# Two short scans form both halves of the LSTM's hidden state; both tanh results share a PSUM bank

## The chip, the cores and the metric

The kernel runs on one core of a Trainium2 chip. The metric is the device time of one execution in microseconds (us). The engines named below are PE (TensorE; its weight loads are shown apart as PEld), DVE (VectorE), ACT (ScalarE) and POOL (GpSimd); SP is the queue that issues most transfers. They run side by side and wait for one another through semaphores.

## The reference, cut to what matters

The model is a chain of four residual layers over 4096 rows of 128 features: a graph layer, a layer with an LSTM, a second graph layer, and attention with a mixture of experts. The change is in the LSTM, which runs over all 4096 rows as one sequence with one batch row:

```python
def step(carry, xp):
    h, c = carry
    gates = xp + h @ W_hh.T
    i, f, g, o = jnp.split(gates, 4, axis=-1)
    c = jax.nn.sigmoid(f) * c + jax.nn.sigmoid(i) * jnp.tanh(g)
    h = jax.nn.sigmoid(o) * jnp.tanh(c)
    return ((h, c), h)
_, hs = jax.lax.scan(step, (h0, c0), jnp.swapaxes(x_proj, 0, 1))   # 4096 steps, 128 units
```

The kernel writes sigmoid(z) as (1 + tanh(z/2))/2. It keeps 2c in `c_twice` and 2h in `hid_t`, with the factors folded into the weights.

## The kernel before

The stages run one after another: norm and messages, `lstm` (lines 334 to 666), the sums over the sequence, the second graph layer, attention, experts. `lstm` holds the recurrence and, beside it, the first graph layer, whose rows are the LSTM's inputs.

**The recurrence.** A unit of h is a partition. h and W_hh are kept in f16 as a high and a low half each; of the four products the three large ones are computed. So step n has, for each of four gates, two matmuls of one column with the high half of h (`wrec` high, `wrec` low) and one with its low half (`wrec` high). They add onto the input's share, which already lies in PSUM (`gates` for i, f, g; `gate_o` apart). The chain of one step is:

- PE, line 431: when the high half is ready, six matmuls for i, f, g and two for o; when the low half is ready, three for i, f, g, which release ACT, and one for o.
- ACT, line 487: tanh of i, f, g into `tanhs`; line 490: tanh of o into `tanh_o` (in SBUF).
- DVE, line 571: the two products of the cell and their sum, `c_twice`, through the accumulator output.
- ACT, line 493: tanh of c into `tanh_c` (in PSUM, in one bank with `c_twice`).
- DVE, line 576: (tanh_o + 1) * tanh_c rounded to f16, the high half; line 578: the same in f32 into `hid_t`; line 582: their difference, the low half; line 585: c kept for the next step.

**Beside it.** After each step every engine runs one piece of the graph layer (`beside`), in a fixed pattern of 16 steps: DVE takes a reciprocal of 52 columns (line 595) in ten of them and a masked product (line 603) in four; ACT an identity, square or exp of 256 columns; PE an f32 matmul (line 454) that accumulates 32 tiles into `acc`. DVE adds a finished tile of `acc` to x (line 609) and goes on to the norm; this work runs 208 steps (`LAG`) ahead of the recurrence. Each engine's order is the program's order; nothing schedules it anew. PSUM's eight banks are all taken: `gates` twice, `gate_o` twice, `acc` twice, `tp`, `c_pair`.

Of the kernel before, what the change touches and what calls it, by code (L numbers as in the profile page):

```python
# [7 lines left out]
F16 = mybir.dt.float16  # L8
I32 = mybir.dt.int32
ACT = mybir.ActivationFunctionType  # L10
# [4 lines left out]
P = 128  # L15
# [309 lines left out]
QUAD = 4  # L325
# [8 lines left out]
def lstm(nc, T):  # L334
# [17 lines left out]
    with Phase(nc, "lstm") as ph:  # L352
# [2 lines left out]
        bias = ph.sb("bias", [P, 4, P])  # L355
        wtmp = ph.sb("wtmp", [P, 4, P])
        tanhs = ph.sb("tanhs", [P, 4])
        tanh_o = ph.sb("tanh_o", [P, 1])
        terms = ph.sb("terms", [P, 2])
        c_pair = ph.ps("c_pair", [P, 2])  # L360
        c_twice, tanh_c = c_pair[:, 0:1], c_pair[:, 1:2]
        warm = ph.sb("warm", [P, 1])
        h_parts = ph.sb("h_parts", [P, NH, 2], F16)
        gates = [ph.ps(f"gates{b}", [P, P, 3]) for b in range(2)]
        gate_o = [ph.ps(f"gate_o{b}", [P, P]) for b in range(2)]
        largest = ph.sb("largest", [P, 2])
# [17 lines left out]
        shifted = ph.sb("shifted", [P, 1], I32)  # L384
        inv = [ph.sb(f"inv{i}", [P, 1]) for i in range(2)]
        sq, left = ph.sb("sq", [P, 1]), ph.sb("left", [P, 1])
        acc = [ph.ps(f"acc{i}", [P, P]) for i in range(2)]
        tp = ph.ps("tp", [P, P])
        loaded = [ph.sem(f"loaded{j}") for j in range(NRING)]
        dist_ready, rec_ready = ph.sem("dist_ready"), ph.sem("rec_ready")  # L390
# [25 lines left out]
        @block.tensor  # L416
        def _(pe):
            def input_gates(t, m):

                k, g = m // 4, m % 4  # L420
                w = (win if k else bias)[:, g, :]
                x = T.xn_t[:, t * P:(t + 1) * P] if k else T.ones[:, :]
                o = gate_o[t % 2][:, :] if g == 3 else gates[t % 2][:, :, g]
                nc.tensor.matmul(o, w, x, start=(k == 0 and g in (0, 3)), stop=False, skip_group_check=True)

            def step(n):
                t, i = divmod(n, P)

                def part(w, g, k):
                    o = gate_o[t % 2][:, i:i + 1] if g == 3 else gates[t % 2][:, i, g:g + 1]  # L430
                    return nc.tensor.matmul(o, wrec[:, w, g, :], h_parts[:, (n - 1) % NH, k:k + 1], start=False,  # L431
                                            stop=True, skip_group_check=True)

                pe.wait_ge(high_ready, n + 1)
                for w in range(2):
                    for g in range(3):
                        part(w, g, 0)
                for w in range(2):
                    part(w, 3, 0)
                pe.wait_ge(low_ready, n + 1)  # L440
                part(0, 0, 1)
                part(0, 1, 1)
                part(0, 2, 1).then_inc(gates_ready, 1)
                part(0, 3, 1).then_inc(gate_o_ready, 1)

            def beside(v):
                q, r = quad_at(v, 2), v % PERIOD
                if q is not None and r < QUAD:
                    t = q // QPT
                    pe.wait_ge(wt_ready, QUAD * q + r + 1)  # L450
                    first = q % QPT == 0 and r == 0
                    if first and t >= 2:
                        pe.wait_ge(x_added, t - 1)
                    nc.tensor.matmul(acc[t % 2][:, :], wt[:, q % 2, r, :], T.msg[:, (q % QPT) * QUAD + r, :],  # L454
                                     start=first, stop=True, skip_group_check=True).then_inc(multiplied, 1)
                t = tile_at(v, 11, 15)
                if t is not None:
                    pe.wait_ge(row_ready, t + 1)
                    if t >= 1:
                        pe.wait_ge(xt_ready, t)  # L460
                    nc.tensor.transpose(tp[:, :], row[:, :], T.ident[:, :]).then_inc(transposed, 1)
                t, i = divmod(v - LAG + 12, P)
                if 0 <= t < NT and i < 8:
                    if i == 0:
                        pe.wait_ge(xt_ready, t + 1)
                        if t >= 2:
                            pe.wait_ge(tanh_o_ready, (t - 1) * P)
                    input_gates(t, i)

            pe.wait_ge(weights_ready, 1)  # L470
            for v in range(LAG + N):
                if v >= LAG:
                    step(v - LAG)
                beside(v)

        @block.scalar
        def _(act):
# [6 lines left out]
            def step(n):  # L484
                t, i = divmod(n, P)
                act.wait_ge(gates_ready, n + 1)
                nc.scalar.activation(tanhs[:, 0:3], gates[t % 2][:, i, :], ACT.Tanh,  # L487
                                     scale=unscale).then_inc(tanhs_ready, 1)
                act.wait_ge(gate_o_ready, n + 1)
                nc.scalar.activation(tanh_o[:, :], gate_o[t % 2][:, i:i + 1], ACT.Tanh,  # L490
                                     scale=unscale).then_inc(tanh_o_ready, 1)
                act.wait_ge(c_ready, n + 1)
                nc.scalar.activation(tanh_c, c_twice, ACT.Tanh, scale=0.5).then_inc(tanh_c_ready, 1)  # L493
# [43 lines left out]
        def _(dve):  # L537
# [22 lines left out]
            s.sync()  # L560
            s.done(nc.vector.tensor_copy(wrec[:, 0, :, :], wtmp[:, :, :]))
            s.done(nc.vector.tensor_tensor(wrec[:, 1, :, :], wtmp[:, :, :], wrec[:, 0, :, :], ALU.subtract))
            nc.vector.memset(c_twice, 0.0).then_inc(weights_ready, 1)
            nc.vector.memset(tanhs[:, 3:4], 0.0).then_inc(c_kept, 1)
            nc.vector.memset(h_parts[:, NH - 1, 0:1], 0.0).then_inc(high_ready, 1)
            nc.vector.memset(h_parts[:, NH - 1, 1:2], 0.0).then_inc(low_ready, 1)

            def step(n):
                dve.wait_ge(tanhs_ready, n + 1)
                dve.wait_ge(c_kept, n + 1)  # L570
                nc.vector.scalar_tensor_tensor(out=terms[:, :], in0=tanhs[:, 0:2], scalar=1.0, in1=tanhs[:, 2:4],  # L571
# [1 line left out]

                dve.wait_ge(tanh_c_ready, n + 1)
                dve.wait_ge(tanh_o_ready, n + 1)
                nc.vector.scalar_tensor_tensor(out=h_parts[:, n % NH, 0:1], in0=tanh_o[:, :], scalar=1.0,  # L576
                                               in1=tanh_c, op0=ALU.add, op1=ALU.mult).then_inc(high_ready, 1)
                nc.vector.scalar_tensor_tensor(out=T.hid_t[:, n:n + 1], in0=tanh_o[:, :], scalar=1.0,  # L578
                                               in1=tanh_c, op0=ALU.add, op1=ALU.mult).then_inc(full_ready, 1)
                dve.wait_ge(full_ready, n + 1)  # L580
                dve.wait_ge(high_ready, n + 2)
                nc.vector.tensor_tensor(h_parts[:, n % NH, 1:2], T.hid_t[:, n:n + 1], h_parts[:, n % NH, 0:1],  # L582
                                        ALU.subtract).then_inc(low_ready, 1)
                dve.wait_ge(c_ready, n + 1)
                nc.vector.tensor_scalar(tanhs[:, 3:4], c_twice, 0.5, None, ALU.mult).then_inc(c_kept, 1)  # L585

            def beside(v):
# [18 lines left out]
                t = tile_at(v, 9, 14)  # L606
                if t is not None:
                    dve.wait_ge(multiplied, (t + 1) * NT)
                    nc.vector.tensor_tensor(T.x[:, t, :], T.x[:, t, :], acc[t % 2][:, :], ALU.add).then_inc(x_added, 1)
                t = tile_at(v, 9, 15)  # L610
                if t is not None:
                    dve.wait_ge(x_added, t + 1)
# [1203 lines left out]
```

## Time and profile before

| | us |
|---|---|
| median of 3 runs (7796.51 to 7797.44) | 7796.72 |
| the profiled execution's own time | 7795.31 |
| its span, first to last instruction | 7793.5 |
| the stretch of the recurrence in it | 108 to 5914 |
| steps of the recurrence | 4096 |

| engine | busy us | share of the span |
|---|---|---|
| PE | 4576.0 | 59% |
| DVE | 5392.0 | 69% |
| ACT | 2826.5 | 36% |
| POOL | 217.1 | 3% |

No engine is full, and within a step the engines take turns. What a step costs is therefore read from the order of starts in one step, and what a piece of it costs from the rows of single instructions.

### The profile page before, as it was taken

To read this page: it belongs to the slowest core of one execution; us is meant where nothing else is said; L and a number is where in the kernel's file an instruction comes from. 1 tells how busy PE (TensorE), PEld (TensorE's weight loads), DVE (VectorE), ACT (ScalarE), POOL (GpSimd) and SP (SyncE) were. 2 spreads that over 40 slices of the span, in tenths; PEclk is the share of its full clock that TensorE was granted. 3 is DMA by queue.
4 is the path that set the end of the run, shared out by engine and by line. 5 is a ranking of instruction groups with operands and counts; after the bars stand their busy time and mean duration, and the time that the engine had idled before them with its cause. 6 is when DMAs were issued, how large, how long until landed. Compare 5 with 4: busy or idle time off the path is not lost. (4 is left out here: it accounts for less than half of the span.)

```text
span 7793.5 us, 179150 instructions
## 1 busy us (share of the span) xinstructions
PE 4576.0 (59%) x57602; PEld 3112.0 (40%) x57632; DVE 5392.0 (69%) x30722; ACT 2826.5 (36%) x14714; POOL 217.1 (3%) x504
## 2 busy tenths in 40 slices
PE   4555555555555555555555555555545958899799
PEld 3444444444444444444444444444433422244344
DVE  7666666666666666666666666666646669999544
ACT  3333333333333333333333333333321000289333
POOL 0000000000000000000000000000000020000111
PEclk6555555555555555555555555555556976699899
DMA  1000000000000000000000000000001810000000
GB/s 45 14 13 14 13 14 14 12 14 13 14 14 12 14 12 14 13 13 14 13 14 13 14 14 12 14 12 14 4 2 66 280 49 0 2 1 1 24 4 5
DMA packets 93263, 164.30 MB, mean 21 GB/s; under 512 B 8711, under 2 KB 23087, under 8 KB 92337
## 3 DMA queue, kind: packets, MB, share of 16 engines
q1 hardware_dynamic: 89009, 150.47, 6.1%
q8 instruction: 442, 7.24, 0.4%
q14 instruction: 484, 3.96, 0.2%
q10 hardware_dynamic: 2816, 2.10, 0.1%
q0 software_dynamic: 512, 0.53, 0.0%
HBM read 146.25 MB, written 2.10 MB: 19 GB/s over the span
## 5 line engine op out<-in xcount | busy, mean ns | idle before, releaser
L431 PE MATMUL lstm_gates<-lstm_h_parts,lstm_wrec 128*128 128x1 f16 x36864 | 2075.8, 170 | 2821.3 <-DVE lstm_h_parts L576 2813.0
L431 PEld LDWEIGHTS lstm_gates<-lstm_h_parts,lstm_wrec 128*128 128x128 f16 x36864 | 1618.8, 107 | 3423.6 <-DVE lstm_h_parts L576 3412.5
L487 ACT ACTIVATE lstm_tanhs<-lstm_gates 128x3 f32<-128x3 f32 x4096 | 708.0, 173 | 2723.0 <-PE lstm_gates L431 2722.8
L431 PE MATMUL lstm_gate_o<-lstm_h_parts,lstm_wrec 128*128 128x1 f16 x12288 | 1440.7, 165 | 0.0
L576 DVE SCALAR_TENSOR_TENSOR lstm_h_parts<-lstm_tanh_o,lstm_c_pair 128x1 f16<-128x1 f32 x4096 | 646.4, 158 | 908.7 <-ACT lstm_c_pair L493 908.7
L571 DVE SCALAR_TENSOR_TENSOR lstm_terms<-lstm_tanhs 128x2 f32<-128x2 f32 x4096 | 659.3, 161 | 765.9 <-ACT lstm_tanhs L487 546.0
L595 DVE RECIPROCAL lstm_rec<-lstm_dist 128x52 f32<-128x52 f32 (+1 forms) x2560 | 1171.8, 462 | 4.2 <-issue 4.2
L493 ACT ACTIVATE lstm_c_pair<-lstm_c_pair 128x1 f32<-128x1 f32 x4096 | 639.0, 156 | 954.3 <-DVE lstm_terms L571 954.3
L431 PEld LDWEIGHTS lstm_gate_o<-lstm_h_parts,lstm_wrec 128*128 128x128 f16 x12288 | 961.1, 104 | 0.0
L454 PE MATMUL lstm_acc<-msg,lstm_wt 128*128 128x128 f32 x2048 | 780.3, 488 | 37.9 <-DVE lstm_wt L603 37.9
L582 DVE TENSOR_TENSOR lstm_h_parts<-hid_t,lstm_h_parts 128x1 f16<-128x1 f32 x4096 | 668.3, 163 | 182.1 <-DVE hid_t L578 13.0
L490 ACT ACTIVATE lstm_tanh_o<-lstm_gate_o 128x1 f32<-128x1 f32 x4096 | 678.4, 166 | 0.0
L585 DVE TENSOR_SCALAR lstm_tanhs<-lstm_c_pair 128x1 f32<-128x1 f32 x4096 | 622.8, 152 | 7.4 <-issue 7.4
L578 DVE SCALAR_TENSOR_TENSOR hid_t<-lstm_tanh_o,lstm_c_pair 128x1 f32<-128x1 f32 x4096 | 607.2, 148 | 0.0
L571 DVE DVE_READ_ACCUMULATOR lstm_terms<-lstm_tanhs 128x1 f32 x4096 | 583.6, 142 | 0.0
L454 PEld LDWEIGHTS lstm_acc<-msg,lstm_wt 128*128 128x128 f32 x2048 | 511.8, 312 | 40.7 <-DVE lstm_wt L603 21.4
L1081 DVE TENSOR_REDUCE maxima_part<-maxima_sc 128x1 f32<-128x1024 f32 (+1 forms) x320 | 331.3, 1108 | 7.7 <-remote 5.6
L1315 DVE TENSOR_TENSOR attend_low<-xn_t,attend_high 128x1024 f16<-128x1024 f32 (+1 forms) x288 | 324.2, 1162 | 6.5 <-ACT attend_high L1270 1.5
L1066 PE MATMUL maxima_sc<-ks,qs 96*128 96x512 f16 x576 | 262.5, 562 | 73.6 <-DVE maxima_part L1081 43.6
L1265 ACT ACTIVATE xn_t<-attend_sc 128x1024 f32<-128x1024 f32 (+1 forms) x288 | 280.6, 985 | 57.3 <-PE attend_sc L1197 25.6
L603 DVE SCALAR_TENSOR_TENSOR lstm_wt<-lstm_dist,lstm_sens 128x128 f32<-128x128 f32 x1024 | 295.4, 291 | 4.6 <-issue 4.6
L1496 PE MATMUL experts_up<-experts_f,experts_w 128*128 128x512 f16 (+1 forms) x1152 | 276.9, 385 | 25.1 <-DVE experts_hidden L1616 24.4
(261 smaller groups left out, 4585.1 us busy)
## 6 DMA issues: line engine op xcount, KB each, us to landing
lstm_ring<-in_adj SPq DMA_DIRECT2D x256, 256.0 KB, 2.7
gnn_ring<-in_adj SPq DMA_DIRECT2D x64, 1024.0 KB, 5.3
w<-in_w SPq DMA_DIRECT2D x2, 1364.0 KB, 9.9
heads_cos<-in_cos SPq DMA_DIRECT2D x8, 256.0 KB, 3.1
heads_sin<-in_sin SPq DMA_DIRECT2D x8, 256.0 KB, 3.6
qs<-heads_q_high SPq DMA_DIRECT2D x64, 32.0 KB, 2.3
out<-x SPq DMA_DIRECT2D x8, 256.0 KB, 2.3
ks<-heads_k_high ACTq DMA_DIRECT2D x16, 64.0 KB, 2.4
```

What stands on the lines that cost most here:

```text
L431: return nc.tensor.matmul(o, wrec[:, w, g, :], h_parts[:, (n - 1) % NH, k:k + 1], start=False, stop=True, skip_group_check=True)
L454: nc.tensor.matmul(acc[t % 2][:, :], wt[:, q % 2, r, :], T.msg[:, (q % QPT) * QUAD + r, :], start=first, stop=True, skip_group_check=True) ...
L487: nc.scalar.activation(tanhs[:, 0:3], gates[t % 2][:, i, :], ACT.Tanh, scale=unscale).then_inc(tanhs_ready, 1)
L490: nc.scalar.activation(tanh_o[:, :], gate_o[t % 2][:, i:i + 1], ACT.Tanh, scale=unscale).then_inc(tanh_o_ready, 1)
L493: nc.scalar.activation(tanh_c, c_twice, ACT.Tanh, scale=0.5).then_inc(tanh_c_ready, 1)
L571: nc.vector.scalar_tensor_tensor(out=terms[:, :], in0=tanhs[:, 0:2], scalar=1.0, in1=tanhs[:, 2:4], op0=ALU.add, op1=ALU.mult, accum_out=c ...
L576: nc.vector.scalar_tensor_tensor(out=h_parts[:, n % NH, 0:1], in0=tanh_o[:, :], scalar=1.0, in1=tanh_c, op0=ALU.add, op1=ALU.mult).then_in ...
L578: nc.vector.scalar_tensor_tensor(out=T.hid_t[:, n:n + 1], in0=tanh_o[:, :], scalar=1.0, in1=tanh_c, op0=ALU.add, op1=ALU.mult).then_inc(fu ...
L582: nc.vector.tensor_tensor(h_parts[:, n % NH, 1:2], T.hid_t[:, n:n + 1], h_parts[:, n % NH, 0:1], ALU.subtract).then_inc(low_ready, 1)
L585: nc.vector.tensor_scalar(tanhs[:, 3:4], c_twice, 0.5, None, ALU.mult).then_inc(c_kept, 1)
L595: nc.vector.reciprocal(rec[:, q % 2, c], dist[:, q % 3, c]).then_inc(rec_ready, 1)
L1081: nc.vector.reduce_max(part[:, k % 2, h, c:c + 1], sc[u % 3][:, 0:w, :].rearrange("p a s -> p (a s)"), AX.X).then_inc(reduced, 1)
```

## The change

The high half and the low half of h become one scan each, over two columns, on DVE. A scan computes state = (data0 * state) - data1 along the row, from the initial value 1.0, and writes every state. With data0 = [tanh_o, tanh_c]:

- the first scan has data1 = [-1, 0]: its states are tanh_o + 1 and (tanh_o + 1) * tanh_c, and the second one, in f16, is the high half;
- the second scan has data1 = [-1, high half]: its second state is (tanh_o + 1) * tanh_c minus the high half, the low half.

For that, tanh_o and tanh_c lie side by side in one PSUM bank (`tanh_pair`), and `c_twice` in one of its own (`c_sum`). The bank is taken from `acc`, which has one buffer now: PE's first matmul of tile t waits for x_added of tile t-1. `h_parts` has five columns a step: a spare one, the constant -1, the high half, a spare one, the low half. The f32 value `hid_t` is computed behind the low half, by a tensor_scalar with tanh_c as its second scalar. ACT's tanh of o waits for `full_ready` of the step before, because `hid_t` reads the bank. On PE the two matmuls of gate o with the high half move behind those that release ACT's first tanh. Three small memsets set up the constants.

```diff
-        tanh_o = ph.sb("tanh_o", [P, 1])
-        c_pair = ph.ps("c_pair", [P, 2])
-        c_twice, tanh_c = c_pair[:, 0:1], c_pair[:, 1:2]
+        c_sum, tanh_pair = ph.ps("c_sum", [P, 1]), ph.ps("tanh_pair", [P, 2])
+        c_twice, tanh_o, tanh_c = c_sum[:, :], tanh_pair[:, 0:1], tanh_pair[:, 1:2]
+        one_less = ph.sb("one_less", [P, 2])
-        h_parts = ph.sb("h_parts", [P, NH, 2], F16)
+        h_parts = ph.sb("h_parts", [P, NH, 5], F16)
-        acc = [ph.ps(f"acc{i}", [P, P]) for i in range(2)]
+        acc = ph.ps("acc", [P, P])
...
                 pe.wait_ge(high_ready, n + 1)
                 for w in range(2):
                     for g in range(3):
                         part(w, g, 0)
-                for w in range(2):
-                    part(w, 3, 0)
                 pe.wait_ge(low_ready, n + 1)
                 part(0, 0, 1)
                 part(0, 1, 1)
                 part(0, 2, 1).then_inc(gates_ready, 1)
+                for w in range(2):
+                    part(w, 3, 0)
                 part(0, 3, 1).then_inc(gate_o_ready, 1)
...
-                    if first and t >= 2:
-                        pe.wait_ge(x_added, t - 1)
+                    if first and t >= 1:
+                        pe.wait_ge(x_added, t)
...
                 act.wait_ge(gate_o_ready, n + 1)
-                nc.scalar.activation(tanh_o[:, :], gate_o[t % 2][:, i:i + 1], ACT.Tanh,
+                if n >= 1:
+                    act.wait_ge(full_ready, n)
+                nc.scalar.activation(tanh_o, gate_o[t % 2][:, i:i + 1], ACT.Tanh,
                                      scale=unscale).then_inc(tanh_o_ready, 1)
...
                 dve.wait_ge(tanh_c_ready, n + 1)
                 dve.wait_ge(tanh_o_ready, n + 1)
-                nc.vector.scalar_tensor_tensor(out=h_parts[:, n % NH, 0:1], in0=tanh_o[:, :], scalar=1.0,
-                                               in1=tanh_c, op0=ALU.add, op1=ALU.mult).then_inc(high_ready, 1)
-                nc.vector.scalar_tensor_tensor(out=T.hid_t[:, n:n + 1], in0=tanh_o[:, :], scalar=1.0,
-                                               in1=tanh_c, op0=ALU.add, op1=ALU.mult).then_inc(full_ready, 1)
-                dve.wait_ge(full_ready, n + 1)
+                nc.vector.tensor_tensor_scan(out=h[:, 0:3:2], data0=tanh_pair[:, :], data1=one_less[:, :], initial=1.0,
+                                             op0=ALU.mult, op1=ALU.subtract).then_inc(high_ready, 1)
                 dve.wait_ge(high_ready, n + 2)
-                nc.vector.tensor_tensor(h_parts[:, n % NH, 1:2], T.hid_t[:, n:n + 1], h_parts[:, n % NH, 0:1],
-                                        ALU.subtract).then_inc(low_ready, 1)
+                nc.vector.tensor_tensor_scan(out=h[:, 3:5], data0=tanh_pair[:, :], data1=h[:, 1:3], initial=1.0,
+                                             op0=ALU.mult, op1=ALU.subtract).then_inc(low_ready, 1)
+                nc.vector.tensor_scalar(T.hid_t[:, n:n + 1], tanh_o, 1.0, tanh_c, ALU.add, ALU.mult).then_inc(full_ready, 1)
                 dve.wait_ge(c_ready, n + 1)
                 nc.vector.tensor_scalar(tanhs[:, 3:4], c_twice, 0.5, None, ALU.mult).then_inc(c_kept, 1)
```

On DVE, in a step of the recurrence with a reciprocal beside it, the rows stood like this before (`lstm_` and a tile's name; the waits are the semaphores above):

```order
L571 SCALAR_TENSOR_TENSOR lstm_terms,lstm_c_pair<-lstm_tanhs 128x2 [waits lstm_c_kept,lstm_tanhs_ready]
L576 SCALAR_TENSOR_TENSOR lstm_h_parts<-lstm_tanh_o,lstm_c_pair 128x1 [waits lstm_tanh_o_ready,lstm_tanh_c_ready]
L578 SCALAR_TENSOR_TENSOR hid_t<-lstm_tanh_o,lstm_c_pair 128x1
L582 TENSOR_TENSOR lstm_h_parts<-hid_t,lstm_h_parts 128x1 [waits lstm_high_ready,lstm_full_ready]
L585 TENSOR_SCALAR lstm_tanhs<-lstm_c_pair 128x1 [waits lstm_c_ready]
L595 RECIPROCAL lstm_rec<-lstm_dist 128x52 [waits lstm_dist_ready]
```

The same place now; lines 582 and 585 are the two scans, which this view names by their instruction's family:

```order
L577 SCALAR_TENSOR_TENSOR lstm_terms,lstm_c_sum<-lstm_tanhs 128x2 [waits lstm_c_kept,lstm_tanhs_ready]
L582 SCALAR_TENSOR_TENSOR lstm_h_parts<-lstm_tanh_pair,lstm_one_less 128x2 [waits lstm_tanh_o_ready,lstm_tanh_c_ready]
L585 SCALAR_TENSOR_TENSOR lstm_h_parts<-lstm_tanh_pair,lstm_h_parts 128x2 [waits lstm_high_ready]
L587 TENSOR_SCALAR hid_t<-lstm_tanh_pair 128x1
L589 TENSOR_SCALAR lstm_tanhs<-lstm_c_sum 128x1 [waits lstm_c_ready]
L599 RECIPROCAL lstm_rec<-lstm_dist 128x52 [waits lstm_dist_ready]
```

The instruction that writes `hid_t` has moved from between the two halves to behind them, and the low half waits for the high half alone.

On PE, the matmuls of one step before:

```order
L431 MATMUL lstm_gates<-lstm_h_parts,lstm_wrec 128x1 [waits lstm_high_ready]
L431 MATMUL lstm_gates<-lstm_h_parts,lstm_wrec 128x1 x5
L431 MATMUL lstm_gate_o<-lstm_h_parts,lstm_wrec 128x1 x2
L431 MATMUL lstm_gates<-lstm_h_parts,lstm_wrec 128x1 [waits lstm_low_ready]
L431 MATMUL lstm_gates<-lstm_h_parts,lstm_wrec 128x1 x2
L431 MATMUL lstm_gate_o<-lstm_h_parts,lstm_wrec 128x1
```

and now:

```order
L431 MATMUL lstm_gates<-lstm_h_parts,lstm_wrec 128x1 [waits lstm_high_ready]
L431 MATMUL lstm_gates<-lstm_h_parts,lstm_wrec 128x1 x5
L431 MATMUL lstm_gates<-lstm_h_parts,lstm_wrec 128x1 [waits lstm_low_ready]
L431 MATMUL lstm_gates<-lstm_h_parts,lstm_wrec 128x1 x2
L431 MATMUL lstm_gate_o<-lstm_h_parts,lstm_wrec 128x1 x3
```

The two matmuls of gate o with the high half stand behind the wait for the low half and behind the three that release ACT.

## Rows read from the trace of the kernel before

**Rows 1.** Busy time by stretch: us, each engine's busy us (instructions), clock, DMA share, GB/s
```profile
108.00:5914.00 5806.00, 2981.51 (x51643) 2376.56 (x51641) 3932.43 (x28197) 2127.51 (x13776) 71.15 (x372) 0.50 0.04 13
```

**Rows 2.** One step in order of time: start us, us, engine, line, operation [idle before]
```profile
2001.67 0.17 ACT L487 ACTIVATE lstm_tanhs<-lstm_gates 128x3 f32<-128x3 f32 x1 [0.47 <-PE lstm_gates L431]
2001.74 0.17 ACT L490 ACTIVATE lstm_tanh_o<-lstm_gate_o 128x1 f32<-128x1 f32 x1
2001.88 0.16 DVE L571 SCALAR_TENSOR_TENSOR lstm_terms<-lstm_tanhs 128x2 f32<-128x2 f32 x1
2001.96 0.14 DVE L571 DVE_READ_ACCUMULATOR lstm_terms<-lstm_tanhs 128x1 f32 x1
2002.14 0.16 ACT L493 ACTIVATE lstm_c_pair<-lstm_c_pair 128x1 f32<-128x1 f32 x1 [0.23 <-DVE lstm_terms L571]
2002.33 0.16 DVE L576 SCALAR_TENSOR_TENSOR lstm_h_parts<-lstm_tanh_o,lstm_c_pair 128x1 f16<-128x1 f32 x1 [0.22 <-ACT lstm_c_pair L493]
2002.40 0.15 DVE L578 SCALAR_TENSOR_TENSOR hid_t<-lstm_tanh_o,lstm_c_pair 128x1 f32<-128x1 f32 x1
2002.54 0.24 PEld L431 LDWEIGHTS lstm_gates<-lstm_h_parts,lstm_wrec 128*128 128x128 f16 x6 [0.96 <-DVE lstm_h_parts L576]
...
2002.59 0.16 DVE L582 TENSOR_TENSOR lstm_h_parts<-hid_t,lstm_h_parts 128x1 f16<-128x1 f32 x1
2002.66 0.15 DVE L585 TENSOR_SCALAR lstm_tanhs<-lstm_c_pair 128x1 f32<-128x1 f32 x1
2002.70 0.13 PEld L431 LDWEIGHTS lstm_gate_o<-lstm_h_parts,lstm_wrec 128*128 128x128 f16 x2
...
2002.73 0.47 DVE L595 RECIPROCAL lstm_rec<-lstm_dist 128x52 f32<-128x52 f32 x1
2002.81 0.16 PEld L431 LDWEIGHTS lstm_gates<-lstm_h_parts,lstm_wrec 128*128 128x128 f16 x3
...
2002.91 0.17 PE L431 MATMUL lstm_gate_o<-lstm_h_parts,lstm_wrec 128*128 128x1 f16 x1
2003.09 0.17 ACT L487 ACTIVATE lstm_tanhs<-lstm_gates 128x3 f32<-128x3 f32 x1 [0.79 <-PE lstm_gates L431]
...
2003.29 0.16 DVE L571 SCALAR_TENSOR_TENSOR lstm_terms<-lstm_tanhs 128x2 f32<-128x2 f32 x1
```

**Rows 3.** By source line: count, ns min/median/max, first and last start us
```profile
L487 ACT ACTIVATE lstm_tanhs<-lstm_gates x4096: 172/173/174, 108.7 to 5913.1; 128x3 f32<-128x3 f32 x196
L576 DVE SCALAR_TENSOR_TENSOR lstm_h_parts<-lstm_tanh_o,lstm_c_pair x4096: 157/158/160, 109.4 to 5913.8; 128x1 f16<-128x1 f32 x196
L578 DVE SCALAR_TENSOR_TENSOR hid_t<-lstm_tanh_o,lstm_c_pair x4096: 147/148/156, 109.4 to 5913.9; 128x1 f32<-128x1 f32 x196
L582 DVE TENSOR_TENSOR lstm_h_parts<-hid_t,lstm_h_parts x4096: 161/163/194, 109.6 to 5914.1; 128x1 f16<-128x1 f32 x196
```

**Rows 4.** By source line: scans and other DVE instructions in later stages
```profile
L746 DVE TENSOR_TENSOR_SCAN sums_inc<-sums_w,sums_zero x1: 1224/1224/1224, 5925.4 to 5925.4; 128x512 f32<-128x512 f32 x1
L746 DVE TENSOR_TENSOR_SCAN sums_inc<-sums_w,sums_inc,sums_zero x7: 1284/1284/1284, 5928.2 to 5945.2; 128x512 f32<-128x512 f32 x7
L743 DVE TENSOR_TENSOR sums_w<-sums_cls,hid_t x8: 691/693/693, 5924.7 to 5944.4; 128x512 f32<-128x512 f32 x8
L748 DVE TENSOR_TENSOR sums_cols<-sums_inc,sums_cols x1: 160/160/160, 5946.5 to 5946.5; 128x1 f32<-128x1 f32 x1
L321 DVE TENSOR_SCALAR deg<-gnn_degs x1: 192/192/192, 6241.5 to 6241.5; 128x32 f32<-128x32 f32 x1
L146 DVE TENSOR_SCALAR norm_var<-norm_mv x3: 181/181/182, 21.8 to 6273.6; 128x32 f32<-128x32 f32 x3
```

**Rows 5.** Timeline of DVE in a step with a late reciprocal
```profile
591.83 0.47 DVE L595 RECIPROCAL lstm_rec<-lstm_dist 128x52 f32<-128x52 f32 x1
592.21 0.10 DVE L571 SCALAR_TENSOR_TENSOR lstm_terms<-lstm_tanhs 128x2 f32<-128x2 f32 x1
592.23 0.14 DVE L571 DVE_READ_ACCUMULATOR lstm_terms<-lstm_tanhs 128x1 f32 x1
```

More of the change, by code:

```diff
@@ L430, in part @@
                     o = gate_o[t % 2][:, i:i + 1] if g == 3 else gates[t % 2][:, i, g:g + 1]
-                    return nc.tensor.matmul(o, wrec[:, w, g, :], h_parts[:, (n - 1) % NH, k:k + 1], start=False,
+                    return nc.tensor.matmul(o, wrec[:, w, g, :], h_parts[:, (n - 1) % NH, 2 * k + 2:2 * k + 3], start=False,
                                             stop=True, skip_group_check=True)
@@ L451, in beside @@
                     first = q % QPT == 0 and r == 0
-                    if first and t >= 2:
-                        pe.wait_ge(x_added, t - 1)
-                    nc.tensor.matmul(acc[t % 2][:, :], wt[:, q % 2, r, :], T.msg[:, (q % QPT) * QUAD + r, :],
+                    if first and t >= 1:
+                        pe.wait_ge(x_added, t)
+                    nc.tensor.matmul(acc[:, :], wt[:, q % 2, r, :], T.msg[:, (q % QPT) * QUAD + r, :],
                                      start=first, stop=True, skip_group_check=True).then_inc(multiplied, 1)
@@ L562, in _ @@
             s.done(nc.vector.tensor_tensor(wrec[:, 1, :, :], wtmp[:, :, :], wrec[:, 0, :, :], ALU.subtract))
+            s.done(nc.vector.memset(h_parts[:, :, :], -1.0))
+            s.mark(nc.vector.memset(one_less[:, 0:1], -1.0))
+            s.done(nc.vector.memset(one_less[:, 1:2], 0.0))
             nc.vector.memset(c_twice, 0.0).then_inc(weights_ready, 1)
             nc.vector.memset(tanhs[:, 3:4], 0.0).then_inc(c_kept, 1)
-            nc.vector.memset(h_parts[:, NH - 1, 0:1], 0.0).then_inc(high_ready, 1)
-            nc.vector.memset(h_parts[:, NH - 1, 1:2], 0.0).then_inc(low_ready, 1)
+            nc.vector.memset(h_parts[:, NH - 1, 2:3], 0.0).then_inc(high_ready, 1)
+            nc.vector.memset(h_parts[:, NH - 1, 4:5], 0.0).then_inc(low_ready, 1)
             def step(n):
+                h = h_parts[:, n % NH, :]
                 dve.wait_ge(tanhs_ready, n + 1)
@@ L608, in beside @@
                     dve.wait_ge(multiplied, (t + 1) * NT)
-                    nc.vector.tensor_tensor(T.x[:, t, :], T.x[:, t, :], acc[t % 2][:, :], ALU.add).then_inc(x_added, 1)
+                    nc.vector.tensor_tensor(T.x[:, t, :], T.x[:, t, :], acc[:, :], ALU.add).then_inc(x_added, 1)
                 t = tile_at(v, 9, 15)
```

## The prediction, as it was put on record before the changed kernel ran

> **What bounds the kernel now.** Read the busy time by stretch first [rows 1]: the recurrence takes 5806 of the span's 7793.5 us, and in it no engine is busy for more than 68% (DVE, 3932 of 5806). Then the starts of line 487 [rows 3]: 4096 of them from 108.7 to 5913.1 us, so one step every 1.417 us. Since the next step needs this step's h, the time of the stage is 4096 times the length of one loop through the engines. A nanosecond taken out of that loop is 4.1 us of the kernel; an instruction beside the loop is free as long as it ends in time.
>
> Now follow one loop in the order of starts [rows 2], from one line 487 (2001.67) to the next (2003.09), 1.42 us. ACT's tanh of i, f, g to line 571: 0.21. Line 571 with its accumulator read to line 493: 0.26. Line 493 to line 576: 0.19. Line 576 to line 582: 0.26. Line 582 to PE's second batch of weight loads (2002.81): 0.22. That batch to line 487: 0.28. The sum is 1.42, so these pieces are the whole loop. Two things to see: the first batch on PE (2002.54) is off the loop, since the second starts only when the low half is there; and DVE's work beside (the reciprocal, 2002.73 to 2003.20) ends 0.09 before line 571 starts again. No wait for a transfer stands in the loop.
>
> **What the change takes out.** From the start of line 576 to the end of line 582, three DVE instructions stand one behind the other: line 578 starts 0.073 after line 576 (2002.33 to 2002.40; DVE overlaps neighbours that don't wait), takes 0.148 [rows 3], line 582 starts some 0.044 behind its end (2002.40 + 0.15 to 2002.59 [rows 2]), because it waits for it, and takes 0.163 [rows 3]. Together 0.428. After the change there are two: scan, wait, scan. The wait is of the same kind, 0.044. So the saving per step is 0.428 - 0.044 - 2d = 0.384 - 2d, with d the time of a two-column scan.
>
> **What a two-column scan costs.** No row shows one. The long one shows 1224 ns for 512 columns from a constant start [rows 4]. A tensor_tensor takes 693 for 512 columns and 160 for one, so (693 - 160)/511 = 1.04 ns a column and 159 ns fixed. If a scan takes two such slots a column, 512 of them are 1068 ns and 156 remain; two columns then make 156 + 4 = 160. That the fixed part comes out beside that of the tensor_tensor is what speaks for the split; one size alone can't show it. The Trainium skill, "DVE: opcode table, instruction layouts, handler registers and perf-mode slots", section Datapath and trigger behaviour, says that the built-in scan runs at half throughput; by that the split is as I took it, and no run here shows it yet.
>
> Two things can be added. The source is PSUM: 11 ns at 32 columns (192 against 181 [rows 4]). The result is f16: line 576 takes 158 and line 578, which differs in that and in being queued behind it, 148 [rows 3], so 10 at most. The dear end is 160 + 11 + 10 = 181. The cheap end is 160 without either, since line 576 has both a PSUM source and an f16 result at 158. I take 164, near the cheap end: lines 576 and 582 (158 and 163) are the rows nearest to the new instructions, in source, result and size. The saving is then 0.384 - 0.328 = 0.056 us a step, 229 us in all; by the cheap end 0.064, 262 us; by the dear end 0.022, 90 us.
>
> A rule of the Trainium skill speaks against it. "VectorE: DVE Perf Modes", section on the TRN2 errata, prices a VectorE instruction at 58 cycles and the columns from SBUF and 120 from PSUM; at its clock of 0.96 GHz the difference is an estimate of 65 ns. Only the low half changes its source that way, and by it the sum would be a loss of 0.009 a step, 7834 us. The rows here show 11 ns, not 65.
>
> **What moves, and what hides it.** Five points, each priced at nothing.
>
> PE's two matmuls of gate o go behind the three that release ACT. Weight loads follow one another at 0.16/6 = 0.027 (2002.54, six, then 2002.70 [rows 2]), so gate o is ready 0.055 later. Its matmul ends at 2003.08 now, level with line 487; ACT's tanh of o starts 0.07 behind line 487 anyway. It would start about 0.10 behind and end at 0.27, with DVE needing it 0.65 behind line 487 (2001.67 to 2002.33). The cover is 0.38. ACT's new wait for `full_ready` of the step before is long met, and behind it only line 493 is queued, 0.47 after line 487.
>
> In return PE is free sooner. The low half would come 0.056 earlier, so the second batch at 2002.75. The six loads of the first batch are through at 2002.70; with the two of gate o still there they would be at 2002.76. So the move is worth up to 0.01, and the rest would be lost only if the low half came another 0.05 earlier.
>
> `hid_t` now stands between the low half and the reciprocal: 0.07 of DVE's queue, or 0.13 if its pointer scalar costs what it does for the scan (1284 against 1224 [rows 4]). The reciprocal would start 0.21 to 0.27 after the low scan (now 0.14 after line 582) and end at 0.68 to 0.74, where line 571's successor is due at 0.70. It can queue: in a step with a late reciprocal line 571 started 0.09 before the end of it and its accumulator read came 0.02 behind that, not 0.08 [rows 5]. So nothing is late until the reciprocal ends 0.85 after the low scan; at least 0.11 are left.
>
> `acc` with one buffer: DVE adds tile t to x at its step 128t + 158 (line 609's place in the pattern), and PE starts tile t+1 at 128t + 160. A step of 1.4 us lies between, so this wait is met. The memsets run once, under 1 us.
>
> **The sum.** The profiled execution took 7795.3, the median is 7796.7; the difference is 1.4 us and I put the saving on the median: 7796.7 - 229 = 7567.7, forecast 7568.
>
> **Rivals.** (1) *The scan has a start-up that the long row hides*, at both scans. The point from which the kernel is slower is d = 192, 28 above my value. For it: the scan of this trace does have dearer starts, 60 ns more where the initial value is a column [rows 4]; and one size leaves the split open. Against: here the initial value is a constant. With 60 ns on each scan the step is 0.448 - 0.384 = 0.064 longer, 262 us: 8059. (2) *PSUM is dear for the low scan.* It decides at 56 ns above my value; with as much as 60, the largest extra in [rows 4], the loss is 0.004 a step, 16 us: 7813. Against it stands the 11 ns. This is the mechanism of the errata table of "VectorE: DVE Perf Modes" in the Trainium skill. (3) *No difference*: scans at 190 to 194 each, which the rows neither show nor forbid: 7797. (4) *A larger gain*: the scans are as short as line 578's 148 (same operands, f32). Then 0.384 - 0.296 = 0.088, of which PE's first batch cuts off what is over 0.056 + 0.05: nothing. 360 us: 7436. Line 576 speaks against it for the first scan, and line 582's 163 for the second.
>
> **How the numbers follow.** Forecast, both scans between 160 and 181: 0.78. Larger gain: 0.06. A gain under 90 us but over 0.2%: 0.04. Within 0.2% (about 16 us, what a measurement of this kernel can tell from no change): 0.04. Slower by (1): 0.05, by (2): 0.03. Faster is 0.78 + 0.06 + 0.04 = 0.88, slower 0.08. The bounds of d give 7535 to 7707; rounded to 7530 to 7705, the range holds the forecast's 0.78 and little else.
>
> **What would show it.** In the changed trace: two scans of about 164 ns; 0.21 from one's start to the other's; the second batch on PE 0.05 behind the low scan's end; the step at 1.361 us; line 487 waiting for the `gates` as before. Wrong would be: scans of 180 or more, line 577 starting behind a reciprocal in most steps (DVE has become the bound), the first scan waiting for tanh of o, or PE's second batch following the first without a gap.

## The result and the profile after

| | before | after |
|---|---|---|
| median, us | 7796.72 | 7526.89 |
| lowest to highest of 4 runs | 7796.51 to 7797.44 | 7523.06 to 7528.89 |
| the profiled execution's own time | 7795.31 | 7527.26 |
| its span | 7793.5 | 7525.4 |
| one step of the recurrence, ns | 1417.4 | 1351.5 |

The ratio is 0.9653 (95% interval 0.9636 to 0.967): 270 us less, where 229 were forecast, and 3 us below the low end of the range. The direction and the place were right; the size was not.

All of it lies in the recurrence. By source line, line 487 of the changed kernel (count, ns min/median/max, first and last start us):

```profile
L487 ACT ACTIVATE lstm_tanhs<-lstm_gates x4096: 172/173/173, 110.5 to 5645.0; 128x3 f32<-128x3 f32 x196
```

From the first start to the last are 4095 steps: (5645.0 - 110.5)/4095 = 1.3515 us, against 1.4174 by [rows 3]. The difference of 65.9 ns times 4096 is 270 us.

One step of the changed kernel in order of time (start us, us, engine, line, operation), which answers to [rows 2]; rows of work beside it are left out, and the view merges PE's two batches into one row of nine loads (the seventh starts 61 ns behind the sixth, where loads without a gap follow at 27):

```profile
2001.47 0.17 ACT L487 ACTIVATE lstm_tanhs<-lstm_gates 128x3 f32<-128x3 f32 x1 [0.40 <-PE lstm_gates L431]
2001.55 0.16 ACT L492 ACTIVATE lstm_tanh_pair<-lstm_gate_o 128x1 f32<-128x1 f32 x1
2001.67 0.16 DVE L577 SCALAR_TENSOR_TENSOR lstm_terms<-lstm_tanhs 128x2 f32<-128x2 f32 x1
2001.76 0.14 DVE L577 DVE_READ_ACCUMULATOR lstm_terms<-lstm_tanhs 128x1 f32 x1
2001.93 0.16 ACT L495 ACTIVATE lstm_tanh_pair<-lstm_c_sum 128x1 f32<-128x1 f32 x1 [0.23 <-DVE lstm_terms L577]
...
2002.12 0.17 DVE L582 TENSOR_TENSOR_SCAN lstm_h_parts<-lstm_tanh_pair,lstm_one_less 128x2 f16<-128x2 f32 x1 [0.22 <-ACT lstm_tanh_pair L495]
2002.33 0.16 DVE L585 TENSOR_TENSOR_SCAN lstm_h_parts<-lstm_tanh_pair,lstm_h_parts 128x2 f16<-128x2 f32 x1
2002.34 0.35 PEld L431 LDWEIGHTS lstm_gates<-lstm_h_parts,lstm_wrec 128*128 128x128 f16 x9 [0.49 <-DVE lstm_h_parts L582]
...
2002.40 0.21 DVE L587 TENSOR_SCALAR hid_t<-lstm_tanh_pair 128x1 f32<-128x1 f32 x1
2002.53 0.15 DVE L589 TENSOR_SCALAR lstm_tanhs<-lstm_c_sum 128x1 f32<-128x1 f32 x1
2002.60 0.47 DVE L599 RECIPROCAL lstm_rec<-lstm_dist 128x52 f32<-128x52 f32 x1
2002.62 0.16 PEld L431 LDWEIGHTS lstm_gate_o<-lstm_h_parts,lstm_wrec 128*128 128x128 f16 x3
...
2002.82 0.17 ACT L487 ACTIVATE lstm_tanhs<-lstm_gates 128x3 f32<-128x3 f32 x1 [0.41 <-PE lstm_gates L431]
2002.90 0.16 ACT L492 ACTIVATE lstm_tanh_pair<-lstm_gate_o 128x1 f32<-128x1 f32 x1
2003.03 0.16 DVE L577 SCALAR_TENSOR_TENSOR lstm_terms<-lstm_tanhs 128x2 f32<-128x2 f32 x1
```

From line 487 to the first scan nothing has changed: 0.65 here (2001.47 to 2002.12), 0.66 in [rows 2]. From there to the low half's start it is 0.21 where it was 0.26.

The two scans and `hid_t` on the page of the changed kernel (count, busy us, mean ns, idle us just before them):

```profile
L582 DVE TENSOR_TENSOR_SCAN lstm_h_parts<-lstm_tanh_pair,lstm_one_less 128x2 f16<-128x2 f32 x4096 | 677.1, 165 | 909.3 <-ACT lstm_tanh_pair L495 909.3
...
L587 DVE TENSOR_SCALAR hid_t<-lstm_tanh_pair 128x1 f32<-128x1 f32 x4096 | 868.6, 212 | 0.0
...
L585 DVE TENSOR_TENSOR_SCAN lstm_h_parts<-lstm_tanh_pair,lstm_h_parts 128x2 f16<-128x2 f32 x4096 | 664.5, 162 | 139.4 <-DVE lstm_h_parts L582 0.2
```

The scans take 165 and 162, where 164 each was taken. But the idle time ahead of the low half is 139.4/4096 = 34 ns, where the prediction put 44. The same row of the kernel before, which the prediction didn't show:

```profile
L582 DVE TENSOR_TENSOR lstm_h_parts<-hid_t,lstm_h_parts 128x1 f16<-128x1 f32 x4096 | 668.3, 163 | 182.1 <-DVE hid_t L578 13.0
```

182.1 against 139.4 is 43 us, where 270 - 229 = 41 are missing. Of the 182.1, 13.0 are 33 single stalls of some 0.35 us on top of the usual gap (33 of the 4096 steps, as the view by source line counts them). So the question for the runs was what set that wait.

### The profile page after: what moved, and what is told of

Read it like the earlier page. It is cut to its first block and busy times, and to the rows that moved or that the text cites. A ratio compares the mean times of both kernels' runs of the same rounds, so it can differ in the third digit from the quotient of the medians.

```text
span 7525.4 us, 179183 instructions
## 1 busy us (share of the span) xinstructions
PE 4512.9 (60%) x57632; PEld 3044.0 (40%) x57632; DVE 5588.1 (74%) x30725; ACT 2830.9 (38%) x14714; POOL 217.7 (3%) x504
## 5 line engine op out<-in xcount | busy, mean ns | idle before, releaser
L431 PE MATMUL lstm_gates<-lstm_h_parts,lstm_wrec 128*128 128x1 f16 x36864 | 1786.0, 170 | 2623.1 <-DVE lstm_h_parts L582 2623.0
L431 PEld LDWEIGHTS lstm_gates<-lstm_h_parts,lstm_wrec 128*128 128x128 f16 x36864 | 1451.4, 107 | 3222.6 <-DVE lstm_h_parts L582 3222.4
L582 DVE TENSOR_TENSOR_SCAN lstm_h_parts<-lstm_tanh_pair,lstm_one_less 128x2 f16<-128x2 f32 x4096 | 677.1, 165 | 909.3 <-ACT lstm_tanh_pair L495 909.3
L495 ACT ACTIVATE lstm_tanh_pair<-lstm_c_sum 128x1 f32<-128x1 f32 x4096 | 639.0, 156 | 938.2 <-DVE lstm_terms L577 938.2
L431 PE MATMUL lstm_gate_o<-lstm_h_parts,lstm_wrec 128*128 128x1 f16 x12288 | 894.2, 165 | 0.0
L587 DVE TENSOR_SCALAR hid_t<-lstm_tanh_pair 128x1 f32<-128x1 f32 x4096 | 868.6, 212 | 0.0
L585 DVE TENSOR_TENSOR_SCAN lstm_h_parts<-lstm_tanh_pair,lstm_h_parts 128x2 f16<-128x2 f32 x4096 | 664.5, 162 | 139.4 <-DVE lstm_h_parts L582 0.2
L431 PEld LDWEIGHTS lstm_gate_o<-lstm_h_parts,lstm_wrec 128*128 128x128 f16 x12288 | 644.3, 104 | 0.0
L492 ACT ACTIVATE lstm_tanh_pair<-lstm_gate_o 128x1 f32<-128x1 f32 x4096 | 639.0, 156 | 6.9 <-issue 6.9
L589 DVE TENSOR_SCALAR lstm_tanhs<-lstm_c_sum 128x1 f32<-128x1 f32 x4096 | 606.4, 148 | 0.0
```

Source lines behind the costliest of these rows:

```text
L492: nc.scalar.activation(tanh_o, gate_o[t % 2][:, i:i + 1], ACT.Tanh, scale=unscale).then_inc(tanh_o_ready, 1)
L582: nc.vector.tensor_tensor_scan(out=h[:, 0:3:2], data0=tanh_pair[:, :], data1=one_less[:, :], initial=1.0, op0=ALU.mult, op1=ALU.subtract). ...
L585: nc.vector.tensor_tensor_scan(out=h[:, 3:5], data0=tanh_pair[:, :], data1=h[:, 1:3], initial=1.0, op0=ALU.mult, op1=ALU.subtract).then_in ...
L587: nc.vector.tensor_scalar(T.hid_t[:, n:n + 1], tanh_o, 1.0, tanh_c, ALU.add, ALU.mult).then_inc(full_ready, 1)
```

## What sets the wait ahead of the low half

Theory W: DVE's low half had two waits in the kernel before and has one now. One of two rides on the instruction; the other, the one written second, is an instruction of its own in DVE's queue and blocks it until its semaphore comes. In the trace's record of the queue's own instructions, in the step of [rows 2], that wait, for the high half, came 39 ns after the high half's end and took 21, and the low half started 44 later: 104 after the high half. Theory F adds that the stalls come with a second wait. The rival, P: the kind of instruction decides, a scan from PSUM against a tensor_tensor from SBUF.

### The kernel before with one wait

```diff
                 dve.wait_ge(full_ready, n + 1)
-                dve.wait_ge(high_ready, n + 2)
                 nc.vector.tensor_tensor(h_parts[:, n % NH, 1:2], T.hid_t[:, n:n + 1], h_parts[:, n % NH, 0:1],
```

> The kernel before with the low half (line 582) waiting for hid_t alone; hid_t is written behind the high half on the same engine. Theory W: no separate wait instruction; the low half starts 34 ns after hid_t's end, 97 after the high half's end where it was 104: 7 ns a step, 29 us; and if the 33 stalls came with the second wait (theory F) 12 us more: 7756 us, without that 7768 us. Rival P: a tensor_tensor from SBUF starts 42 ns after its wait: 7797 us, or 7785 us if only the stalls go.

Measured: 7752.93 us, ratio 0.9942 (0.9925 to 0.9958), 45 less. The low half on its page:

```profile
L581 DVE TENSOR_TENSOR lstm_h_parts<-hid_t,lstm_h_parts 128x1 f16<-128x1 f32 x4096 | 666.6, 163 | 140.5
```

The same tensor_tensor from SBUF now starts 140.5/4096 = 34 ns after `hid_t`, as the scan does, and the row names no stalls. P falls. From here to the changed kernel it is 7752.9 - 7526.9 = 226 us, and that is what the prediction's sum had priced at 229.

### The kernel before with its two waits swapped

```diff
-                dve.wait_ge(full_ready, n + 1)
                 dve.wait_ge(high_ready, n + 2)
+                dve.wait_ge(full_ready, n + 1)
```

> The kernel before with the two waits of the low half (line 582) written the other way round, so that the wait for hid_t is the separate instruction. Theory W: the low half starts 39 + 21 + 44 = 104 ns after hid_t's end where it starts 41 after it now: 63 more a step, 258 us, 8055 us. Rival: the order of two waits doesn't matter, 7797 us.

Measured in one run: 8045.54 us, 248 more. On its page:

```profile
L582 DVE TENSOR_TENSOR lstm_h_parts<-hid_t,lstm_h_parts 128x1 f16<-128x1 f32 x4096 | 667.5, 163 | 438.0 <-DVE hid_t L578 15.1
```

Without the stalls, (438.0 - 15.1)/4063 = 104 ns stand ahead of the low half, counted from the end of `hid_t`. The same two waits in the other order cost 63 ns more at this place, and 248/4096 = 61 ns a step in all. So the kernel before had its waits in the better order: the separate wait, for the high half, came earlier and cost 7 ns of 42.

### The changed kernel with a second wait, written first and written second

The added wait is for `hid_t` of the step before, which has long been made. Written first, it makes the wait for the high half the separate one:

```diff
+                if n >= 1:
+                    dve.wait_ge(full_ready, n)
                 dve.wait_ge(high_ready, n + 2)
```

> The changed kernel with one wait more ahead of the low scan: on hid_t of the step before (met long ago), written ahead of the wait for the high half. Theory W (the way of waiting): of two waits one rides on the instruction and the other, the one written second, is an instruction of its own on DVE that blocks its queue; in the kernel before, the low half started 104 ns after the high half's end for that reason, 39 to that wait, 21 for it, 44 to the start. Here the wait for the high half becomes that instruction, so the low scan should start 104 ns after the high scan's end where it starts 34 after it now: 70 ns more a step, 287 us, 7814 us. Rival P (the kind of instruction: a scan from PSUM starts sooner after its wait than a tensor_tensor from SBUF): the added wait is met, 34 ns stay, 7527 us.

Measured: 7823.87 us, ratio 1.0032 (1.002 to 1.0045): 26 us above the kernel before, which took 7797.47 beside it. On its page:

```profile
L587 DVE TENSOR_TENSOR_SCAN lstm_h_parts<-lstm_tanh_pair,lstm_h_parts 128x2 f16<-128x2 f32 x4096 | 665.6, 163 | 430.7 <-DVE lstm_h_parts L582 14.6
```

(430.7 - 14.6)/4064 = 102 ns ahead of the low scan, where 34 were. One wait that is always met takes the whole gain away, because it makes the other one block the queue.

Written second, it is itself the separate one:

```diff
                 dve.wait_ge(high_ready, n + 2)
+                if n >= 1:
+                    dve.wait_ge(full_ready, n)
```

> The same added wait, but written behind the one for the high half, so that by theory W the met wait is the separate instruction and the wait for the high half rides on the scan: the low scan should start 34 to 36 ns after the high scan's end, 7527 to 7535 us. By a third theory, F, the 33 stalls of 0.35 us that the kernel before had just ahead of the low half come with any second wait at that place: then some 12 us come back, 7539 us, with gaps of about 0.39 us ahead of the low scan. Rival P: 7527 us.

Measured: 7535.05 us (7534.04 to 7536.01), ratio 0.9662 (0.9646 to 0.9678), 8 above the changed kernel. On its page:

```profile
L587 DVE TENSOR_TENSOR_SCAN lstm_h_parts<-lstm_tanh_pair,lstm_h_parts 128x2 f16<-128x2 f32 x4096 | 666.1, 163 | 146.7 <-DVE lstm_h_parts L582 8.6
```

The gap is 34 again, (146.7 - 8.6)/4064, and 8.6 us in 32 stalls are back. The 8 us of the whole kernel agree with that, but alone they would show little: one kernel differed by as much between two chips (7515.98 and 7524.07 us, below). So both theories hold here: the order of the waits sets the gap, and a second wait at this place brings the stalls with it.

The traces also show where the stalls fall. Count all rows of DVE's queue, the separate waits included: any two of the 33 stalls of the kernel before are a multiple of 128 rows apart. Whenever the low half stands on such a row behind a separate wait, it stalls: 33 of 33 times in the kernel before and in the one with its waits swapped, 32 of 32 times in each of the two with the added wait. With one wait it stands there about as often and stalls hardly ever: none of 30 times in the kernel before with one wait, 1 of 30 in the changed kernel. What happens at every 128th row, no run shows.

## The other steps of the prediction

### PE's two matmuls of gate o put back

```diff
                     for g in range(3):
                         part(w, g, 0)
+                for w in range(2):
+                    part(w, 3, 0)
                 pe.wait_ge(low_ready, n + 1)
...
-                for w in range(2):
-                    part(w, 3, 0)
                 part(0, 3, 1).then_inc(gate_o_ready, 1)
```

> The changed kernel with PE's two matmuls of gate o with the high half put back ahead of the wait for the low half. The prediction gave their move up to 10 ns a step. In the changed trace the sixth load stands 61 ns ahead of the second batch; two loads more at 27 each leave 7 where a load needs 27, so the second batch should start some 20 ns later: 82 us, 7609 us, and PE should show no gap between the batches. Rival: PE's second batch is held by the low half alone (it is ready 53 ns after the low scan's end): 7527 us.

Measured: 7594.97 us, ratio 0.9738 (0.9721 to 0.9754), 68 above the changed kernel. PE's loads and the low scan in one step (timeline):

```profile
2002.82 0.16 DVE L585 TENSOR_TENSOR_SCAN lstm_h_parts<-lstm_tanh_pair,lstm_h_parts 128x2 f16<-128x2 f32 x1
2002.84 0.24 PEld L431 LDWEIGHTS lstm_gates<-lstm_h_parts,lstm_wrec 128*128 128x128 f16 x6 [0.97 <-DVE lstm_h_parts L582]
...
2003.00 0.13 PEld L431 LDWEIGHTS lstm_gate_o<-lstm_h_parts,lstm_wrec 128*128 128x128 f16 x2
...
2003.05 0.16 PEld L431 LDWEIGHTS lstm_gates<-lstm_h_parts,lstm_wrec 128*128 128x128 f16 x3
```

The second batch follows the first without a gap (2003.00 and two loads at 0.027), 0.07 after the low scan's end (2002.82 + 0.16) where 0.05 is due. With the low half this early, PE's first batch would have become the bound: the move is worth 68/4096 = 17 ns a step, more than the 10 that the prediction allowed it.

### `hid_t` between the scans

The line of `hid_t` is written between the two scans, and nothing else is changed.

> The changed kernel with hid_t (the tensor_scalar with the pointer scalar) put between the two scans, where it stood in the kernel before. The low scan doesn't wait for its result. Theory D (what cost was that the low half waited for hid_t's result, not that hid_t stood in between): hid_t is issued 80 ns after the high scan and holds DVE's queue for 131 ns, so the low scan starts 211 ns after the high scan where it starts 199 now: 12 ns a step, 49 us, 7576 us. Rival (the place costs its whole duration, 212 ns behind the high scan's start of queueing, and a wait): about 80 + 212 + 34 = 326 where it is 199, 127 ns, 520 us, 8047 us.

Measured: 7515.98 us on one chip, and 7524.07 (7520.17 to 7526.0) on a second one, where the changed kernel took 7526.59 (7525.37 to 7529.06): no loss, and a gain that is hardly clear of the spread. The expectation on that second chip:

> The kernel with hid_t between the scans once more, on the chip of the runs beside it, to tell its 11 us below the changed kernel from the spread between chips: 7516 us if they are its own, 7527 us if not.

> The changed kernel as it stands, on the chip of the two runs beside it, as their reference: 7527 us.

The low scan on the page of the first of these runs:

```profile
L586 DVE TENSOR_TENSOR_SCAN lstm_h_parts<-lstm_tanh_pair,lstm_h_parts 128x2 f16<-128x2 f32 x4096 | 625.5, 153 | 0.0
```

It does start some 10 ns later, queued behind `hid_t`, but takes 153 where it took 162, so it ends when it did. Theory D holds in its mechanism, and its 49 us of loss didn't come. Moving `hid_t` out of the way earned nothing; that the low half no longer waits for its result did: here the low half starts 208 ns after the high half (median of 4096), and in the kernel before with one wait 255 ns, though `hid_t` took 148 there and takes 212 here.

### The pair in SBUF, and the high half without a scan

```diff
-        c_sum, tanh_pair = ph.ps("c_sum", [P, 1]), ph.ps("tanh_pair", [P, 2])
+        c_sum, tanh_pair = ph.ps("c_sum", [P, 1]), ph.sb("tanh_pair", [P, 2])
```

> The changed kernel with tanh_pair in SBUF where it is in PSUM; nothing else. By the rows ACT's tanh takes 166 ns into SBUF and 156 into PSUM, so the tanh of c on the loop costs 10 more; if a PSUM source costs a scan the 11 ns that line 321 shows at 32 columns, both scans are 11 shorter each: 12 less, 49 us, 7478 us with the 10 taken off (10 - 22 = -12). If a PSUM source costs nothing at two columns: 10 more, 41 us, 7568 us. If PSUM is dear by 60 ns a scan (the rival of the prediction): 110 less, 450 us, 7077 us.

Measured: 7596.62 us, ratio 0.9742 (0.9725 to 0.9758), 70 above the changed kernel. By source line, ACT's tanh of c and the two scans:

```profile
L495 ACT ACTIVATE lstm_tanh_pair<-lstm_c_sum x4096: 171/171/173, 109.4 to 5712.9; 128x1 f32<-128x1 f32 x196
L582 DVE TENSOR_TENSOR_SCAN lstm_h_parts<-lstm_tanh_pair,lstm_one_less x4096: 164/165/175, 109.6 to 5713.1; 128x2 f16<-128x2 f32 x196
L585 DVE TENSOR_TENSOR_SCAN lstm_h_parts<-lstm_tanh_pair,lstm_h_parts x4096: 160/164/166, 109.8 to 5713.3; 128x2 f16<-128x2 f32 x196
```

The scans take what they took from PSUM, within 2 ns. ACT pays: 171 into SBUF where it takes 156 into PSUM, 15 ns where the expectation had 10, and 15 times 4096 = 61 of the 70 us. The Trainium skill, "ScalarE: Activation LUTs", section Step-by-step: what each stage is for, says that PSUM is the faster destination for ACT; the trace agrees, with these 15 ns. The other 9 us stand in the busy times of the two scans, 678.9 + 671.8 us here against 677.1 + 664.5.

With the pair in SBUF the high half can be one scalar_tensor_tensor as it was before:

```diff
-                nc.vector.tensor_tensor_scan(out=h[:, 0:3:2], data0=tanh_pair[:, :], data1=one_less[:, :], initial=1.0,
-                                             op0=ALU.mult, op1=ALU.subtract).then_inc(high_ready, 1)
+                nc.vector.scalar_tensor_tensor(out=h[:, 2:3], in0=tanh_o, scalar=1.0,
+                                               in1=tanh_c, op0=ALU.add, op1=ALU.mult).then_inc(high_ready, 1)
```

> As the kernel with tanh_pair in SBUF, and the high half made by one scalar_tensor_tensor of one column where it is a scan of two. By the rows that instruction took 158 ns (line 576 before) and the scan 165: 7 less a step, 29 us below the kernel with the pair in SBUF and both scans. If the scan's two columns cost nothing over one column: equal to it.

Measured: 7583.26 us (7574.39 to 7588.58), 13 below the kernel with the pair in SBUF and both scans, and 56 above the changed kernel. It took 163 ns where the scan took 165 or 166, not 158: two ns, not seven. So the scan costs two or three ns a step more than the one-column instruction that it replaces here. Why that instruction takes 163 where line 576 took 158, no run shows.

### Scans of 1 to 512 columns

The changed kernel with DVE instructions ahead of the recurrence, each waiting for the one in front of it: scans from SBUF to f32 (line 572) and to f16 (line 578), from PSUM to f16 (line 576), and tensor_tensor (line 574).

> The changed kernel with a measurement ahead of the recurrence, three times over: scans of 1, 2, 4, 8, 32, 128 and 512 columns from SBUF to f32 and to f16, from PSUM to f16 up to 128, each beside a tensor_tensor of the same width. The prediction's split: 156 ns fixed and 2.09 ns a column, so 158, 160, 165, 173, 223, 423 and 1224 ns to f32. Rival (a start-up that the long row hides): 180 or more at two columns, and a smaller slope. PSUM and f16 by the prediction's bounds: 0 to 11 and 0 to 10 ns more. Total time some 60 us more, not used.

Measured (one run, 7549.84 us), groups by shape in the stretch from 50 to 110 us (count, busy us, mean ns, idle):

```profile
L572 DVE TENSOR_TENSOR_SCAN lstm_probe<-lstm_bias,lstm_wtmp 128x512 f32<-128x512 f32 x3 | 3.7, 1224 | 0.1
...
L574 DVE TENSOR_TENSOR lstm_probe<-lstm_bias,lstm_wtmp 128x512 f32<-128x512 f32 x3 | 2.1, 691 | 0.1
...
L572 DVE TENSOR_TENSOR_SCAN lstm_probe<-lstm_bias,lstm_wtmp 128x128 f32<-128x128 f32 x3 | 1.3, 424 | 0.1
...
L574 DVE TENSOR_TENSOR lstm_probe<-lstm_bias,lstm_wtmp 128x32 f32<-128x32 f32 x3 | 0.6, 192 | 0.1
...
L578 DVE TENSOR_TENSOR_SCAN lstm_probe<-lstm_bias,lstm_wtmp 128x2 f16<-128x2 f32 x3 | 0.5, 162 | 0.1
...
L572 DVE TENSOR_TENSOR_SCAN lstm_probe<-lstm_bias,lstm_wtmp 128x2 f32<-128x2 f32 x3 | 0.5, 161 | 0.1
L576 DVE TENSOR_TENSOR_SCAN lstm_probe<-lstm_acc,lstm_wtmp 128x2 f16<-128x2 f32 x3 | 0.5, 161 | 0.1
...
L574 DVE TENSOR_TENSOR lstm_probe<-lstm_bias,lstm_wtmp 128x1 f32<-128x1 f32 x3 | 0.5, 159 | 0.1
```

The split holds: (1224 - 161)/510 = 2.08 ns a column and 157 fixed, twice the tensor_tensor's (691 - 159)/511 = 1.04. That is the half throughput of the Trainium skill's page on DVE's opcode table ("DVE: opcode table, instruction layouts, handler registers and perf-mode slots", section Datapath and trigger behaviour). At two columns neither PSUM nor f16 costs anything: 161, 162, 161. The 65 ns that the prediction estimated from the errata table of the Trainium skill ("VectorE: DVE Perf Modes", section on the TRN2 errata) don't show here, and the gap ahead of a scan is 34 ns from either memory (the kernel with the pair in SBUF has 139.4 us of idle time there too).

### Fewer waits

```diff
                 dve.wait_ge(tanh_c_ready, n + 1)
-                dve.wait_ge(tanh_o_ready, n + 1)
...
                 act.wait_ge(gate_o_ready, n + 1)
-                if n >= 1:
-                    act.wait_ge(full_ready, n)
```

Both in the kernel with `hid_t` between the scans.

> As the kernel with hid_t between the scans, and two second waits taken out that a later wait implies: DVE's for tanh of o ahead of the high scan (ACT makes tanh of c after it) and ACT's for full_ready (the gates come from the low half, which DVE makes after hid_t). Theory F (stalls of some 0.35 us sit at second waits): the stalls of 0.27 us ahead of ACT's tanh of o go, and those on the loop, 1.9 us in sum with hid_t between, don't grow; the step's median stays 1353 ns. 7510 to 7516 us. Rival (each separate wait holds the queue for its 21 ns): 10 to 20 ns less a step, 7434 to 7475 us.

Measured: 7520.33 us (7518.74 to 7526.53), on the second chip, where its neighbours took 7524.07 and 7526.59. ACT's idle time ahead of tanh of o, 6.9 us in the changed kernel, is gone:

```profile
L490 ACT ACTIVATE lstm_tanh_pair<-lstm_gate_o 128x1 f32<-128x1 f32 x4096 | 639.0, 156 | 0.0
```

That was off the loop, and the step hardly changes. Its ratio, 0.9647 (0.9633 to 0.966), and that of the changed kernel beside it, 0.9653 (0.964 to 0.9667), overlap: the lowest median of that chip's three, 6 us below the changed kernel, but not shown to be faster. A separate wait that is met early costs nothing on the loop that these runs can tell; the rival's 10 to 20 ns fall.

## Why the prediction was wrong, point by point

**The bound.** Right: the time of the stage is 4096 times the loop, and 270 us are 4096 times 65.9 ns. The step is 1.3515 us, where 1.361 was forecast.

**The mis-sized term.** The step that failed is the wait ahead of the low half: "The wait is of the same kind, 0.044." It was not, and it took 0.034 after the change; the 10 ns times 4096 are 41 us, and 229 + 41 = 270. Before, the low half waited for two semaphores, and the separate wait for the high half, not the end of `hid_t`, set its start; now one wait rides on the instruction. The 0.044, given as read from two starts in a timeline (which show 0.04), is the mean of the row, 182.1/4096 = 44.5 ns: 34 that one wait takes, 7 for the separate wait and 3 for the stalls. With 34 on the side of after and the row's 44.5 on that of before, the saving would have been 0.073 + 0.148 + 0.0445 + 0.163 - 0.034 - 0.328 = 0.0665 a step, 272 us, where 270 were measured. The kernel before with one wait shows the part by itself: 45 us, and the rest of the change 226.

The 34 could be read from the kernel before. Its line 317, in a later stage, waits for one semaphore, that of the DVE instruction in front of it (count, busy us, mean ns, idle us just before):

```profile
L317 DVE TENSOR_TENSOR gnn_dsum<-gnn_dsum,gnn_pair 128x1024 f32<-128x1024 f32 x56 | 68.6, 1225 | 1.9
```

1.9/56 = 34 ns.

**The bounds.** They took in d, the part that was right, and not the wait, which was treated as known. A wait between two instructions is a term with bounds of its own: 34 to 44, both from rows of the kernel before, would have put the low end at 7494.

**The scan.** Right: 165 and 162, and the split is measured. That the mean came within 1 ns of the 164 is luck in part, since the argument left 160 to 181. The reading that a PSUM source or f16 costs up to 11 and 10 is not borne out at two columns (161, 162, 161), and at 32 columns a tensor_tensor from SBUF takes 192, as long as line 321 from PSUM. What took 10 ns off line 578 [rows 3] was then probably that it stood queued, as the low scan does behind `hid_t`; no run takes line 578 out of the queue.

**What moves.** `hid_t`, now with a pointer scalar, takes 212 and holds the queue 0.13 (2002.40 to 2002.53), as the dear case had it, and line 577 still starts 0.21 after line 487: covered. Tanh of o starts 0.08 behind line 487, and is covered. PE's move was taken as up to 10 ns and is 17, because the low half comes still earlier than forecast. The single buffer of `acc` makes PE wait once, 2.9 us for line 613 at about 96 us, ahead of the recurrence, and not within it. The recurrence starts 1.8 us later (110.5 against 108.7 us); no run takes that apart.

**The rivals.** A start-up of the scan and a dear PSUM source are both refuted by the scans of 1 to 512 columns. That the change makes no difference is out by the result. The larger gain was priced with a shorter scan, 360 us; the scans were not shorter, and the 41 us above the forecast came from the wait.

## What to carry to other kernels

In a loop that several engines run in turns, count the waits of each instruction on it and not only its time. On DVE, where the runs show it: give an instruction on the loop one wait where a later one implies an earlier, and where it needs two, write the one that is met last first, so that it rides on the instruction. Before a short dependent chain is rewritten, look for the value that is only needed later (`hid_t`) and take it out of the dependency, not necessarily out of its place. Where such a chain gets shorter, look at the engine behind it too: here PE's queue had to be cleared by 17 ns for the gain to arrive.

## What the runs showed of the hardware that was not expected

- The order of two waits on one DVE instruction is worth 63 ns at its place (438.0 against 182.1 us of idle time over 4096 steps, 8045.54 against 7796.72 us in all), and a wait that is always met can cost 68 ns (102 against 34), by making the other one a separate, blocking one.
- Single stalls stand at second waits: 33 of 0.39 us with the usual gap ahead of the low half in the kernel before (13.0 us), 32 of 0.27 with the met wait written second (8.6 us). All of them fall on places a multiple of 128 rows apart in DVE's queue, and the low half stalls whenever it stands on such a place behind a separate wait. ACT's tanh of o in the changed kernel does the same in ACT's queue: 38 of 38 times, 6.9 us of idle time, which is gone without its second wait. The cause is open.
- The same scan on DVE shows about 10 ns less time where it stands queued directly behind another instruction (153 against 162).
